# First graph's step tables built between the blocks of the first projection

## The chip, the cores and the metric

The kernel runs on one core of a Trainium2 chip. The metric is the device time of one execution, in microseconds (us); the kernel before has a median of 3173.57 us over three runs.

## The reference, cut to what matters

Two layers of a graph network on 3125 nodes with 256 features. In the first half of layer 0 the node features are normed, projected to q, k, v, and used both for an attention over 53125 sorted edges and for a mixer whose per-head k and v are normed over 64 features.

```python
edge_index = jnp.stack([src, dst])
xn = _layernorm(x, axis=-1)
x = x + _L0_gnn_ref(xn, edge_index, Wq, bq, Wk, bk, Wv, bv, Ws, bs) + _L0_mix_ref(xn[None], Wqkv, Wout, bout)[0]
...
# in _L0_gnn_ref
alpha = jnp.einsum('ehc,ehc->eh', q[dst], k[src]) / jnp.sqrt(jnp.float32(C))
amax = jax.ops.segment_max(alpha, dst, num_segments=n)
ex = jnp.exp(alpha - amax[dst])
out = jax.ops.segment_sum(msg, dst, num_segments=n)
```

The rest (an expert layer, a second graph layer, a second mixer and a gated expert layer with a second edge list) follows in order and is not touched, but for one helper that the second edge list uses too.

## The kernel before

The 3125 nodes lie as NB = 25 blocks of 128 rows in `k.X`. The sorted edges are cut into chunks of 128 and, by the block of 128 nodes to which they belong, into T1 "steps" in G1 = 4 groups of 128. For each step the kernel needs a small table: which chunk, which block, each edge's node relative to its block (`e.rel`, and as rows in memory, `e.rel_rows`), its source node (`e.src`), where a node's run of edges starts and ends (`e.flags_tab`, `e.link_tab`), and which places are void (`e.hole`). Class `Steps` makes them, and only the attention, after the projection, reads them.

Each part of the program is a `Block`: every engine has its own written-out instruction stream, and all engines meet at the Block's end. The parts at the start come in this order.

`Loads` (Block at L529): ACT issues two DMAs for x and then 28 for weights and biases. Its end is the end of the issues, not of the transfers.

`first_steps` (L295 to 326): SP loads the last node of each of the 416 chunks (`load`, L187). DVE turns it into a row of end steps (`count`), TensorE widens that row over 128 partitions (`widen`, L211), DVE compares and reduces it into chunk and block numbers (`cuts`, L242 to 252), GpSimd issues 12 indirect DMAs that fetch the edges (`gather`, L225), and SP stores and reads back the block numbers (`store`, L193, L196). DVE meanwhile takes the 25 layer statistics (`stats.block`, L469), waits for the edges and makes the flags (`mark`, L258 to 275). SP stores rows, flags and links (L199 to 205) and waits for all of them. TensorE turns two tables (`flip`, L217), and DVE keeps them (`settle`, L281 to 292).

`turn_weights` (L549 to 577): 36 weight tiles of 128x128 are transposed by TensorE and copied by DVE through eight PSUM banks. TensorE waits first for all weight loads.

`stats.finish` (L481 to 497) makes the node scales. `project0` (L586 to 784) then goes over the 25 blocks. In one turn TensorE multiplies q, k, v of a block (L694), transposes the next normed block (L677), multiplies the mixer's k and v (L704), and adds the last block to the dot products (L682). ACT squares (L632), takes a root (L635) and norms the next block (L582). DVE adds the biases into a ring of five (`qkv`, L758 and L759), keeps the transposed block (`xT`, L748), reduces the squares (L763) and scales the k heads (L770), after which it raises `heads`. GpSimd splits q in three (L664 to 668), and SP stores k and v (L647). The `Chain` class gives each DVE instruction of a chain a wait on the one before.

TensorE's q, k, v product of a block needs that block kept and the adds of the block before:

```python
pe.wait_ge(kept, b + 2)
pe.wait_ge(ab_used, b + 1)
```

The second edge list's tables are made by the same `Steps` inside `combine1` (L2361 to 2476). There `mark` stands whole between the fourth and fifth group of blocks, and TensorE's `flip` waits for it before its own fifth group.

Of the kernel before, what the change touches and what calls it, by code (L numbers as in the profile page):

```python
# [6 lines left out]
F32 = mybir.dt.float32  # L7
# [6 lines left out]
P = 128  # L14
# [141 lines left out]
class Steps:  # L156


    def __init__(self, nc, s, k, name, pairs, chunks, groups, e):
        self.nc, self.k, self.pairs, self.chunks, self.groups, self.e = nc, k, pairs, chunks, groups, e  # L160
        self.last_i = s.sb(name + "last_i", [1, chunks], I32)
        self.last_b = s.sb(name + "last_b", [1, chunks], I32)
        self.end_step = s.sb(name + "end_step", [1, chunks])
        self.below = s.sb(name + "below", [P, groups, chunks])
# [3 lines left out]
        self.here = s.sb(name + "here", [P, 2, groups, P])  # L168
        self.near = s.sb(name + "near", [P, 2, groups, P])
        self.rel_t = s.sb(name + "rel_t", [P, groups, P])  # L170
        self.rel_h = s.sb(name + "rel_h", [P, groups, P], BF)
        self.tmp = s.sb(name + "tmp", [P, groups, P])
# [3 lines left out]
        if self.block_row is None:  # L176
            self.block_row = s.sb(name + "block_row", [1, groups * P], I32)
        if e.flags_tab is not None:
            self.valid, self.starts, self.ends = (s.sb(name + x, [P, groups, P]) for x in ("valid", "starts", "ends"))
# [10 lines left out]
    def store(self, sp):  # L190
        e, groups = self.e, self.groups
# [5 lines left out]
        sp.wait_ge(self.blocked, 16)  # L197
        sp.wait_ge(self.ready, 3)
        sp.dma_start(e.rel_rows.rearrange("(g p) e -> p g e", p=P), self.rel_h[:, :, :]).then_inc(self.bdone, 16)  # L199
        sp.wait_ge(self.bdone, 32)  # L200
        if e.flags_tab is not None:
# [11 lines left out]
    def flip(self, pe):  # L213
        pe.wait_ge(self.cmp_done, 2)
        for j, x in enumerate((self.rel_t, self.here[:, 1])):
# [23 lines left out]
    def cuts(self, dve):  # L239
        v, k, c, cut, groups, chunks = self.nc.vector, self.k, self.c, self.cut, self.groups, self.chunks  # L240
        dve.wait_ge(self.spread, 1)
        c.link(v.tensor_tensor(self.below[:, :, :], wide(self.wide_end[:, 0:chunks].unsqueeze(1), [P, groups, chunks]),  # L242
                               wide(k.count_col[:, 0:groups].unsqueeze(2), [P, groups, chunks]), ALU.is_lt))
        c.link(v.tensor_reduce(cut[:, 0], self.below[:, :, :], AX.X, ALU.add))
# [10 lines left out]
    def mark(self, dve):  # L255
        v, c, here, near, tmp, rel_t, valid = self.nc.vector, self.c, self.here, self.near, self.tmp, self.rel_t, self.valid
# [7 lines left out]
        v.tensor_copy(self.rel_h[:, :, :], rel_t[:, :, :]).then_inc(self.ready, 1)  # L264
        c.link(v.tensor_scalar(valid[:, :, :], rel_t[:, :, :], 0.0, None, ALU.is_ge))
        c.link(v.tensor_scalar(tmp[:, :, :], rel_t[:, :, :], float(P), None, ALU.is_lt))
        c.link(v.tensor_tensor(valid[:, :, :], valid[:, :, :], tmp[:, :, :], ALU.mult))
        for flags, j in ((self.starts, 0), (self.ends, 1)):
            c.link(v.tensor_tensor(tmp[:, :, :], here[:, 0], near[:, j], ALU.not_equal))
            c.link(v.scalar_tensor_tensor(out=flags[:, :, :], in0=tmp[:, :, :], scalar=RESET, in1=valid[:, :, :],  # L270
                                          op0=ALU.mult, op1=ALU.mult))
        if self.e.flags_tab is not None:
            for j, x in enumerate((self.starts, self.ends)):
                v.tensor_reduce(self.link[:, j], x[:, :, :], AX.X, ALU.min).then_inc(self.flagged, 1)
        dve.sem_inc(self.cmp_done, 1)

    def settle(self, dve):
        v, c, e, groups = self.nc.vector, self.c, self.e, self.groups
# [3 lines left out]
        if e.step_row is not None:  # L282
# [4 lines left out]
            c.link(v.tensor_tensor(e.step_row[:, :, U:], duo[:, 1], duo[:, 0], ALU.subtract))  # L287
        if e.hole is not None:
# [4 lines left out]


def first_steps(nc, k, pairs, e, stats, got_x):  # L295

    with Scope(nc) as s:
        st = Steps(nc, s, k, "s1_", pairs, C1, G1, e)
        with nc.Block() as block:
            @block.sync  # L300
            def _(sp):
                st.load(sp)
                st.store(sp)

            @block.tensor
            def _(pe):
                st.widen(pe)
                st.flip(pe)

            @block.gpsimd  # L310
            def _(pool):
                st.gather(pool)

            @block.vector
            def _(dve):
                st.count(dve)
                st.cuts(dve)
                dve.wait_ge(got_x, 32)
                for b in range(NB):
                    stats.block(b)  # L320
                st.mark(dve)
                st.settle(dve)
                stats.end(dve)
# [177 lines left out]
class Loads:  # L501


    def __init__(self, nc, s, k, pj, a):
# [3 lines left out]
        self.got_x, self.got_w, cleared = (s.sem(q) for q in ("got_x", "got_w", "cleared"))  # L508
# [40 lines left out]
def turn_weights(nc, k, pj, ld):  # L549

    with Scope(nc) as s:
# [7 lines left out]
        with nc.Block() as block:  # L559
            @block.sync  # L560
            def _(sp):
                sp.wait_ge(ld.got_x, 32)

# [9 lines left out]
            def _(dve):  # L573
                for j, (_x, y) in enumerate(jobs):
                    dve.wait_ge(turned, j + 1)
                    nc.vector.tensor_copy(y, bank[j % 8][:, 0:P]).then_inc(kept, 1)
                dve.wait_ge(kept, len(jobs))

# [7 lines left out]
def project0(nc, k, pj, q_parts, kv_tab):  # L586
# [5 lines left out]
    with Scope(nc) as s:  # L592
# [22 lines left out]
        out = [s.sem(f"p0_out{j}") for j in range(B5)]  # L615
        K8 = MH // 2
        with nc.Block() as block:
# [34 lines left out]
            def _(pool):  # L652
                pool.sem_inc(parted, B5)
                pool.wait_ge(zeroed, 2)
                for i in range(0, NB // B5):
# [5 lines left out]
                    for j in range(B5):  # L661
# [7 lines left out]
                        pool.sem_inc(parted, 1)  # L669

            @block.tensor
            def _(pe):
# [14 lines left out]
                def turn(i, last=False):  # L687
                    for j in range(B5):
# [19 lines left out]
                        product((j - 1) % B5)  # L708
                pe.sem_inc(turned, B5)
# [17 lines left out]
            def _(dve):  # L727
# [22 lines left out]
                def turn(i, first=False, last=False):  # L750
                    c = Chain(dve, chain, i * (PER * B5))
                    for j in range(B5):
# [18 lines left out]
                        dve.sem_inc(heads, 1)  # L771
                    assert c.n == PER * B5
# [2341 lines left out]
def program(nc, a, out):  # L3114
    with Scope(nc) as s:
# [12 lines left out]
        with Scope(nc) as g:  # L3128
            e1 = Graph(g, "e1_", G1, streamed=True)
            with Scope(nc) as t:  # L3130
                q_parts = t.sb("q_parts", [P, NB, 3, D], BF)
                with Scope(nc) as t2:
                    pj = Projection(t2)
                    stats = LayerStats(nc, t2, k, "n0_")
                    with Scope(nc) as t3:
                        ld = Loads(nc, t3, k, pj, a)
                        first_steps(nc, k, a["pairs"], e1, stats, ld.got_x)
                        turn_weights(nc, k, pj, ld)
                    stats.finish()
                    project0(nc, k, pj, q_parts, kv_tab)  # L3140
# [101 lines left out]
```

## Time and profile before

| | |
|---|---|
| median of 3 runs | 3173.57 us (3168.86 to 3176.24) |
| span of the profiled execution | 3169.3 us |
| TensorE, VectorE (DVE), ScalarE (ACT), GpSimd (POOL) busy | 2325.7, 2011.6, 1372.1, 1774.3 us |
| mean granted TensorE clock | 0.856 |
| projection loop, first product to last | about 106.8 to 312 us |

The span runs from the first to the last instruction of one execution, which lies inside the range of the timed runs. Start times in the timeline count from the span's start. A bracket behind a row is the idle time of the engine ahead of it, and what ended it.

### The profile page before, as it was taken

The numbers are of one execution on the slowest core, as the hardware profiler recorded it, in microseconds if no ns is written. First come the engines' busy times: TensorE is split into PE (matmuls) and PEld (weight loads), VectorE is DVE, ScalarE is ACT, GpSimd is POOL, SyncE is SP. The second block draws the span as 40 slices with busy tenths as digits, with TensorE's granted clock in tenths as the row PEclk, the third lists the DMA queues.
The fourth block names the chain that finished last, engine by engine and source line by source line (L and its number), as shares of the span: only waits on it lengthen the run. The fifth ranks groups of instructions, "written<-read, shape, count | busy, mean of one in ns | idle before, by whom it ended". The sixth has DMA issues, their size and how long they took to land. (4 is left out here: it accounts for less than half of the span.)

```text
span 3169.3 us, 41063 instructions
## 1 busy us (share of the span) xinstructions
PE 2325.7 (73%) x11127; PEld 1529.8 (48%) x11128; DVE 2011.6 (63%) x4060; ACT 1372.1 (43%) x3793; POOL 1774.3 (56%) x1789
## 2 busy tenths in 40 slices
PE   0798677777776667669968667777777888888781
PEld 0454455555554556246623323333325676777660
DVE  3444799999998888100136399989995642222588
ACT  0122555655653344311126388888883222222230
POOL 1244788877874125657763377777772057777100
PEclk9899788888888655789979798989998779999895
DMA  5000677667762100034312133333331121111105
GB/s 122 21 34 30 201 206 204 202 205 205 201 204 65 55 18 27 11 111 124 89 50 64 53 97 100 100 102 100 100 94 17 28 57 36 36 36 36 16 1 173
DMA packets 163816, 287.79 MB, mean 91 GB/s; under 512 B 55320, under 2 KB 99357, under 8 KB 163598
## 3 DMA queue, kind: packets, MB, share of 16 engines
q0 software_dynamic: 79568, 187.15, 22.1%
q1 hardware_dynamic: 68628, 75.89, 7.9%
q10 hardware_dynamic: 15402, 22.14, 2.0%
q8 instruction: 102, 1.67, 0.2%
q14 instruction: 116, 0.95, 0.1%
HBM read 248.79 MB, written 36.25 MB: 90 GB/s over the span
## 5 line engine op out<-in xcount | busy, mean ns | idle before, releaser
L2273 POOL DMA_INDIRECT cv_x<-x_tab,e_src x440 | 447.8, 1018 | 197.5 <-issue 91.1
L2286 PE MATMUL cv_ps<-cv_msg,cv_hot 128*128 128x512 f32 x880 | 433.9, 651 | 167.0 <-DVE acc L2336 131.8
L913 POOL DMA_INDIRECT at_kv<-kv_tab,e_src x440 | 472.4, 1074 | 146.4 <-issue 92.0
L2707 POOL DMA_INDIRECT gs_h<-h_tab,fc_q x312 | 296.8, 951 | 178.1 <-issue 93.3
L2286 PEld LDWEIGHTS cv_ps<-cv_msg,cv_hot 128*128 128x128 f32 x880 | 179.2, 210 | 421.4 <-ACT cv_msg L2299 203.3
L1957 POOL DMA_INDIRECT pairs<-gating_pair,gating_place x288 | 278.4, 967 | 158.5 <-issue 68.9
L2299 ACT ACTIVATE cv_msg<-cv_x,factors 128x64 f32<-128x64 f32 x1320 | 356.5, 333 | 0.0
L2336 DVE TENSOR_TENSOR acc<-acc,cv_ps 128x256 f32 x880 | 307.4, 416 | 37.1 <-PE cv_ps L2286 30.5
L2297 ACT ACTIVATE cv_msg<-cv_x,factors 128x256 f32<-128x256 f32 x440 | 217.7, 495 | 130.6 <-DMA cv_x<-x_tab,e_src 130.6
L1049 PE MATMUL at_a<-at_kv,at_hot_e 128*128 128x264 f32 x880 | 251.3, 415 | 7.0 <-DVE at_kv L1122 5.0
L1024 PE MATMUL at_q<-q_parts,at_hot_n 128*128 x1320 | 217.3, 318 | 41.0 <-DVE at_kv L1106 32.2
L2668 ACT ACTIVATE gs_x_hid<-gs_x_h,x_b 128x128 f32<-128x128 f32 x320 | 91.2, 368 | 301.9 <-PE gs_x_h L2635 301.9
L2645 PE MATMUL gs_x_y<-x_w,gs_x_hid 128*128 128x256 f32 x640 | 160.4, 402 | 61.1 <-DVE gs_y L2675 57.5
L1024 PEld LDWEIGHTS at_q<-q_parts,at_hot_n 128*128 128x128 bf16 x1320 | 142.4, 110 | 106.8 <-issue 58.1
L2788 DVE TENSOR_REDUCE gs_as_dst<-gs_d 128x32 f32<-128x96 f32 x39 | 10.1, 258 | 280.0 <-DMA gs_h<-h_tab,fc_q 280.0
L1049 PEld LDWEIGHTS at_a<-at_kv,at_hot_e 128*128 128x128 f32 x880 | 165.9, 209 | 37.2 <-issue 7.3
L1133 DVE TENSOR_TENSOR acc<-acc,at_a 128x528 f32 x220 | 154.2, 701 | 36.1 <-PE at_a L1049 30.2
L2645 PEld LDWEIGHTS gs_x_y<-x_w,gs_x_hid 128*128 128x128 f32 x640 | 122.5, 199 | 82.4 <-ACT gs_x_hid L2668 55.8
L1106 DVE TENSOR_TENSOR at_kv<-at_kv,at_q 128x512 f32<-128x512 f32 x220 | 147.2, 680 | 18.2 <-DMA at_kv<-kv_tab,e_src 9.3
L2635 PE MATMUL gs_x_h<-xnT,x_w 128*128 128x128 f32 x1280 | 156.4, 279 | 0.0
L2635 PEld LDWEIGHTS gs_x_h<-xnT,x_w 128*128 128x128 f32 x1280 | 153.1, 195 | 2.1
L975 ACT ACTIVATE at_away_e<-count_row,e_rel 128x128 f32<-128x128 f32 x440 | 139.0, 386 | 0.1
(548 smaller groups left out, 4601.6 us busy)
## 6 DMA issues: line engine op xcount, KB each, us to landing
x_w<-in_L_ffn_w SPq DMA_DIRECT2D x16, 1024.0 KB, 7.7
at_rel_row<-e_rel_rows SPq DMA_DIRECT2D x55, 256.0 KB, 4.7
experts_out<-gs_y ACTq DMA_DIRECT2D x20, 512.0 KB, 2.7
x_y<-experts_out SPq DMA_DIRECT2D x20, 512.0 KB, 4.8
at_kv<-kv_tab,e_src POOLq DMA_INDIRECT x440, 3.9
cv_x<-x_tab,e_src POOLq DMA_INDIRECT x440, 2.8
kv_tab<-p_qkv SPq DMA_DIRECT2D x25, 256.0 KB, 2.0
gs_h<-h_tab,fc_q POOLq DMA_INDIRECT x312, 2.4
```

What stands on the lines that cost most here:

```text
L913: nc.gpsimd.indirect_dma_start(out=kv[:, t % (RING * Q4), 0:2 * D], out_offset=None, in_=kv_tab, in_offset=bass.IndirectOffsetOnAxis(ap=e. ...
L1024: ins = nc.tensor.matmul(ps_q[dd % 3][:, u, :], hot_n[:, t // Q4 % NHOT, t % Q4 * P:(t % Q4 + 1) * P], q_parts[:, ds(b, 1), n, :].rearrang ...
L1049: nc.tensor.matmul(to, hot_e[:, t // Q4 % NEDGE, t % Q4, :], kv[:, t % (RING * Q4), D:2 * D + H1], start=(u == 0), stop=(u == 1), skip_gro ...
L1957: nc.gpsimd.indirect_dma_start(out=pairs, out_offset=bass.IndirectOffsetOnAxis(ap=place_i[:, c:c + 1], axis=0), in_=pair[:, c, :], in_offs ...
L2273: nc.gpsimd.indirect_dma_start(out=xg[:, i % RT, u, :], out_offset=None, in_=x_tab, in_offset=bass.IndirectOffsetOnAxis(ap=e.src[:, t:t + ...
L2286: nc.tensor.matmul(ps[u % R][:, :], hot[:, i % 2, u, :], msg[:, i % 2, u, :], start=True, stop=True).then_inc(summed, 1)
L2297: nc.scalar.activation(msg[:, h, u, 0:D], xg[:, i % RT, u, :], ACT.Copy, scale=factor[:, t:t + 1, 0])
L2299: ins = nc.scalar.activation(msg[:, h, u, D + m * M:D + (m + 1) * M], xg[:, i % RT, u, 0:M], ACT.Copy, scale=factor[:, t:t + 1, 1 + m])
L2336: v.tensor_tensor(row, row, ps[u % R][:, n * D:(n + 1) * D], ALU.add).then_inc(added, 1)
L2635: ins = self.nc.tensor.matmul(self.ps_h[e % 2][:, f * P:(f + 1) * P], self.x1.w1[:, e, c, f * P:(f + 1) * P], self.xnT[:, c, b * P:(b + 1) ...
L2645: ins = self.nc.tensor.matmul(self.ps_y[e % 2][:, 0:D], self.hid[:, e % 2, f, :], self.x1.w2[:, e, f, :], start=(f == 0), stop=(f == FX // ...
L2707: nc.gpsimd.indirect_dma_start(out=hg[:, i % RT, u, :], out_offset=None, in_=h_tab, in_offset=bass.IndirectOffsetOnAxis(ap=e.src[:, i * U ...
```

## The change

The `first_steps` Block is gone. `turn_weights` takes the 25 statistics at its head on DVE, with a wait for each of five loads of x (six DMAs, for the last block is short), and then the copies. The table work moves into `project0`: `load` at the head of SP's stream, and pieces of the rest behind named blocks of each engine's loop.

The helper's methods are cut up (`cuts` into two, `mark` into four, `settle` into two, `store` into three). `mark` no longer copies three of its four columns of edges to float tiles: it reads the integer columns in place. Some tiles share memory.

```diff
-                act.dma_start(k.X[:, 0:NB - 1, :], a["x"][0:(NB - 1) * P, :].rearrange("(b p) d -> p b d", p=P)).then_inc(got_x, 16)
-                act.dma_start(k.X[0:LAST, NB - 1, :], a["x"][(NB - 1) * P:N, :]).then_inc(got_x, 16)
+                for g in range(NB // B5):
+                    lo, hi = g * B5, min(g * B5 + B5, NB - 1)
+                    act.dma_start(k.X[:, lo:hi, :], a["x"][lo * P:hi * P, :].rearrange("(b p) d -> p b d", p=P)).then_inc(got_x[g], 16)
+                act.dma_start(k.X[0:LAST, NB - 1, :], a["x"][(NB - 1) * P:N, :]).then_inc(got_x[NB // B5 - 1], 16)
...
 # turn_weights, DVE
+                for b in range(NB):
+                    if b % B5 == 0:
+                        dve.wait_ge(ld.got_x[b // B5], 32 if b // B5 == NB // B5 - 1 else 16)
+                    stats.block(b)
...
 # mark
         dve.wait_ge(self.got, 48 * self.groups)
-        v.tensor_copy(near[:, 0], self.edges[0][:, :, :, 0])
-        v.tensor_copy(near[:, 1], self.edges[2][:, :, :, 0])
-        v.tensor_copy(here[:, 1], self.edges[1][:, :, :, 1])
-        c.link(v.tensor_copy(here[:, 0], self.edges[1][:, :, :, 0]))
-        c.link(v.tensor_tensor(rel_t[:, :, :], here[:, 0], wide(self.cut[:, 5].unsqueeze(2), [P, self.groups, P]), ALU.subtract))
+        v.tensor_copy(self.from_node[:, :, :], self.edges[1][:, :, :, 1])
+        c.link(v.tensor_tensor(rel_t[:, :, :], self.edges[1][:, :, :, 0], wide(self.cut[:, 5].unsqueeze(2), [P, self.groups, P]), ALU.subtract))
...
+AT_COUNT, AT_CUTS, AT_MARK = 1, 5, 11
...
 # project0, SP, after the store of block b
+                steps.load(sp)                       # ahead of the loop
+                        if b == AT_CUTS + 2:
+                            steps.store_blocks(sp)
+                        if b == AT_MARK + 1:
+                            steps.store_rows(sp)
+                        if b == AT_MARK + 4:
+                            steps.store_flags(sp)
 # GpSimd, after the split of block b
+                        if b == AT_CUTS + 1:
+                            steps.gather(pool)
 # TensorE, after the dot products in block b
+                        if b == AT_COUNT + 2:
+                            steps.widen(pe)
+                        if b == AT_MARK + 5:
+                            steps.flip(pe)
 # DVE, after it has raised heads for block b
+                        if b == AT_COUNT:
+                            steps.count(dve)
+                        if b == AT_CUTS:
+                            steps.cuts_begin(dve)
+                        if b == AT_CUTS + 1:
+                            steps.cuts_end(dve)
+                        if b == AT_MARK:
+                            steps.mark_rows(dve)
+                        if b == AT_MARK + 1:
+                            steps.mark_valid(dve)
+                        if b == AT_MARK + 2:
+                            steps.mark_flags(dve, 0)
+                        if b == AT_MARK + 3:
+                            steps.mark_flags(dve, 1)
+                        if b == AT_MARK + 6:
+                            steps.settle_rows(dve)
+                        if b == AT_MARK + 7:
+                            steps.settle_holes(dve)
```

## Rows read from the trace of the kernel before

**Rows 1.** Timeline of the loads: start us, us, engine, line, what was issued

```profile
5.75 0.43 ACTq L533 DMA_DIRECT2D X<-in_x  x1
...
29.88 0.64 SPq L187 DMA_DIRECT2D s_last_i<-in_pairs  x1
```

**Rows 2.** Busy time by stretch, the 30th microsecond; last two columns DMA share, GB/s

```profile
29.00:30.00 1.00, 0.00 (x0) 0.00 (x0) 0.00 (x0) 0.00 (x0) 0.00 (x0) 1.00 0.13 28
```

**Rows 3.** Timeline of DVE in first_steps (each row may end in its wait)

```profile
35.42 0.58 DVE L237 TENSOR_TENSOR s_end_step<-s_end_step,count_row 1x416 f32<-1x416 f32 x1
...
37.84 1.89 DVE L242 TENSOR_TENSOR s_below<-s_turned,count_col 128x1664 f32<-128x1664 f32 x1 [1.84 <-PE s_turned L211]
39.77 1.89 DVE L244 TENSOR_REDUCE s_cut<-s_below 128x4 f32<-128x1664 f32 x1
...
42.66 0.16 DVE L252 SCALAR_TENSOR_TENSOR s_cut<-s_cut 128x4 f32<-128x4 f32 x1
42.86 8.26 DVE L469 BATCH_NORM_STATS2 n_parts<-X 128x6 f32<-128x256 f32 x25
...
59.97 0.43 DVE L258 CAST s_near<-s_edges 128x512 f32<-128x512 int32 x1 [8.85 <-DMA s_edges<-in_pairs,e_chunk]
...
67.06 0.69 DVE L274 TENSOR_REDUCE s_link<-s_starts 128x4 f32<-128x512 f32 x1
```

**Rows 4.** Waits of SP's queue up to 110 us: us in total, times, longest

```profile
SPq L299 <- DMA e_link<-s_link: 12.6, 1, 12.6
...
SPq L196 <- DMA s_block_of_step<-s_block_i: 9.7, 1, 9.7
```

**Rows 5.** Timeline of turn_weights and the first instruction of stats.finish

```profile
83.54 3.65 PE L570 MATMUL turn_bank<-ident,mix_kv 128*128 128x128 f32 x16 [14.42 <-PEq L299]
...
89.11 2.46 DVE L576 COPY fcT<-turn_bank 128x128 f32<-128x128 f32 x12
...
92.09 0.20 DVE L487 TENSOR_TENSOR n_t<-n_parts 128x25 f32<-128x25 f32 x1 [0.52 <-PEq L559]
```

**Rows 6.** Line L763 by itself: ns min/median/max, first and last start us

```profile
L763 DVE TENSOR_REDUCE p_st<-p_sq x25: 1219/1220/1221, 117.1 to 307.0; 128x16 f32<-128x1024 f32 x25
```

**Rows 7.** Timeline of one block of the projection

```profile
127.81 0.44 PE L677 MATMUL p_t<-ident,p_xn 128*128 128x128 f32 x2 [0.38 <-ACT p_xn L582]
128.19 3.67 PE L704 MATMUL p_m<-mix_kvT,p_xT 128*128 128x512 f32 x8
...
129.15 0.41 DVE L748 COPY p_xT<-p_t 128x256 f32<-128x256 f32 x1
...
132.59 1.88 PE L694 MATMUL p_a<-Wqkv,p_xT 128*128 128x512 f32 x4
...
132.96 1.22 DVE L763 TENSOR_REDUCE p_st<-p_sq 128x16 f32<-128x1024 f32 x1 [3.40 <-ACT p_sq L632]
```

**Rows 8.** Busy time by stretch: PE, PEld, DVE, ACT, POOL; clock, DMA share, GB/s

```profile
104.00:112.00 8.00, 7.38 (x12) 3.41 (x13) 0.43 (x1) 0.00 (x0) 0.00 (x0) 0.50 0.00 0
...
128.20:136.10 7.90, 7.52 (x27) 4.04 (x27) 3.86 (x8) 2.21 (x4) 3.61 (x5) 1.00 0.09 33
```

**Rows 9.** TensorE's flip in first_steps, its first half

```profile
67.15 1.11 PE L217 MATMUL s_turned<-ident,s_rel_t 128*128 128x128 f32 x4 [29.34 <-DVEq L275]
```

**Rows 10.** Line L225, the gathers on GpSimd: ns min/median/max, first and last start

```profile
L225 POOL DMA_INDIRECT s_edges<-in_pairs,e_chunk x12: 946/946/1104, 42.4 to 56.3; - x12
```

**Rows 11.** Timeline of the attention: a GpSimd gather and a DVE product beside it

```profile
360.07 1.22 DVE L1122 TENSOR_TENSOR at_kv<-at_kv 128x1024 f32<-128x1024 f32 x1
360.25 1.87 POOL L913 DMA_INDIRECT at_kv<-kv_tab,e_src  x1 [0.31 <-issue]
```

**Rows 12.** Timeline of the second edge list's mark and flip

```profile
2480.95 0.34 DVE L258 CAST s_near<-s_edges 128x384 f32<-128x384 int32 x1
...
2482.14 0.56 DVE L262 TENSOR_TENSOR s_rel_t<-s_here,s_cut 128x384 f32<-128x384 f32 x1
...
2486.82 0.90 PE L217 MATMUL s_turned<-ident,s_rel_t 128*128 128x128 f32 x3 [6.66 <-DVEq L275]
```

More of the change, by code:

```diff
@@ L176, in __init__ @@
         if self.block_row is None:
-            self.block_row = s.sb(name + "block_row", [1, groups * P], I32)
+            self.block_row = row
         if e.flags_tab is not None:
-            self.valid, self.starts, self.ends = (s.sb(name + x, [P, groups, P]) for x in ("valid", "starts", "ends"))
+            self.valid = own_valid
+            self.starts, self.ends = (s.sb(name + x, [P, groups, P]) for x in ("starts", "ends"))
         self.turned = [s.ps(name + f"turned{j}", [P, 512]) for j in range(2)]
@@ L190, in store, with store_blocks @@
     def store(self, sp):
-        e, groups = self.e, self.groups
+        self.store_blocks(sp)
+        self.store_rows(sp)
+        self.store_flags(sp)
+    def store_blocks(self, sp):
+        groups = self.groups
         sp.wait_ge(self.ready, 2)
@@ L197, in store, with store_rows @@
         sp.wait_ge(self.blocked, 16)
+    def store_rows(self, sp):
+        e = self.e
         sp.wait_ge(self.ready, 3)
@@ L200, in store, with store_flags @@
         sp.wait_ge(self.bdone, 32)
+    def store_flags(self, sp):
+        e = self.e
         if e.flags_tab is not None:
@@ L214, in flip @@
         pe.wait_ge(self.cmp_done, 2)
-        for j, x in enumerate((self.rel_t, self.here[:, 1])):
+        for j, x in enumerate((self.rel_t, self.from_node)):
             for g in range(self.groups):
@@ L255, in mark, with mark_rows, mark_valid @@
     def mark(self, dve):
[L256 to L262 removed]
+        self.mark_rows(dve)
+        self.mark_valid(dve)
+        for j in range(2):
+            self.mark_flags(dve, j)
+    def mark_rows(self, dve):
+        v, c, rel_t = self.nc.vector, self.c, self.rel_t
+        dve.wait_ge(self.got, 48 * self.groups)
+        v.tensor_copy(self.from_node[:, :, :], self.edges[1][:, :, :, 1])
+        c.link(v.tensor_tensor(rel_t[:, :, :], self.edges[1][:, :, :, 0], wide(self.cut[:, 5].unsqueeze(2), [P, self.groups, P]), ALU.subtract))
         v.tensor_copy(self.rel_h[:, :, :], rel_t[:, :, :]).then_inc(self.ready, 1)
+    def mark_valid(self, dve):
+        v, c, tmp, rel_t, valid = self.nc.vector, self.c, self.tmp, self.rel_t, self.valid
         c.link(v.tensor_scalar(valid[:, :, :], rel_t[:, :, :], 0.0, None, ALU.is_ge))
@@ L267, in mark, with mark_flags, settle_rows @@
         c.link(v.tensor_tensor(valid[:, :, :], valid[:, :, :], tmp[:, :, :], ALU.mult))
[L268 to L271, printed above, removed]
+    def mark_flags(self, dve, j):
+        v, c, tmp, valid = self.nc.vector, self.c, self.tmp, self.valid
+        flags = (self.starts, self.ends)[j]
+        c.link(v.tensor_tensor(tmp[:, :, :], self.edges[1][:, :, :, 0], self.edges[2 * j][:, :, :, 0], ALU.not_equal))
+        c.link(v.scalar_tensor_tensor(out=flags[:, :, :], in0=tmp[:, :, :], scalar=RESET, in1=valid[:, :, :],
+                                      op0=ALU.mult, op1=ALU.mult))
         if self.e.flags_tab is not None:
-            for j, x in enumerate((self.starts, self.ends)):
-                v.tensor_reduce(self.link[:, j], x[:, :, :], AX.X, ALU.min).then_inc(self.flagged, 1)
-        dve.sem_inc(self.cmp_done, 1)
+            v.tensor_reduce(self.link[:, j], flags[:, :, :], AX.X, ALU.min).then_inc(self.flagged, 1)
+        if j == 1:
+            dve.sem_inc(self.cmp_done, 1)
     def settle(self, dve):
+        self.settle_rows(dve)
+        self.settle_holes(dve)
+    def settle_rows(self, dve):
         v, c, e, groups = self.nc.vector, self.c, self.e, self.groups
@@ L292, in settle @@
             c.link(v.tensor_scalar(e.hole[:, :], e.hole[:, :], LOW, None, ALU.mult))
[L295 to L323, printed above, removed]
 def segment_softmax(nc, k, name, groups, heads, score, valid, starts, ends, scale, x1, xnT):
@@ L507, in __init__ @@
         self.fc = [s.sb(f"fc{j}", [P, KC, D]) for j in range(3)]
-        self.got_x, self.got_w, cleared = (s.sem(q) for q in ("got_x", "got_w", "cleared"))
+        self.got_x = [s.sem(f"got_x{g}") for g in range(NB // B5)]
+        self.got_w, cleared = s.sem("got_w"), s.sem("cleared")
         got_x, got_w = self.got_x, self.got_w
@@ L577, in _ @@
                 dve.wait_ge(kept, len(jobs))
+                stats.end(dve)
 def normed_block(nc, k, act, b, slot, sem):
```

37 lines of the change are left out of this document (21 added, 16 removed).

## The prediction, on record before the result

> **What bounds the kernel now.** The page's chain of waits covers only the last part of the span, so I read the start of the program: first the timeline, then the waits of SP's queue, then busy time by stretch. No engine is near full over the whole span, so what counts is which event opens each stretch.
>
> The loads' part ends when SP starts its first DMA, at 29.9 us [rows 1]. By then the transfers are nearly through: in the 30th microsecond the DMA engines are 13% busy [rows 2]. From 29.9 to 83.5 us the tables of the first graph are built, one dependent step after another. DVE is idle 8.85 us for the gathered edges [rows 3], and at the end all engines wait for SP, which waits 12.6 us for the link stores [rows 4]. Only the 25 statistics (8.26 us, [rows 3]) are work that the projection needs. TensorE starts the weight tiles at 83.54, DVE ends them at 89.11 + 2.46 = 91.57, and the node scales start at 92.09 [rows 5].
>
> The projection is a loop with a fixed pitch: (307.0 - 117.1) / 24 = 7.91 us [rows 6]. TensorE is busy 7.52 us in such a stretch, at clock 1.00 (2.4 GHz), and idle 0.38 us a block, waiting for the normed block; DVE is busy 3.86 and GpSimd 3.61 of 7.90 us [rows 7, 8]. TensorE bounds the loop, closely followed by the chain product, square, reduce, root, norm, transpose. DVE and GpSimd have half of each block free.
>
> **Part 1: the removed Block.** Start of the node scales after the change, built up:
>
> - Loads end. ACT issues four DMAs more, at most 4 x 0.43 = 1.7 us [rows 1]. The bytes are the same, and they fill the time to the 29th microsecond anyway, so the lower bound is 0. I take 0.5: the issues run beside the transfers. 29.9 + 0.5 = 30.4.
> - Statistics: 8.26 us, to 38.7. The five waits on x cost nothing: x was issued first, and all transfers are nearly done at 30 [rows 2]. For the same reason the split of x gains nothing, since the statistics cannot start before the loads' Block ends.
> - Weight tiles: before, 91.57 - 83.54 = 8.03 us from TensorE's first transpose to DVE's last copy [rows 5]. Now TensorE fills the eight banks while DVE takes the statistics, so only the copies are left: the last 12 took 2.46 us, 0.205 each, and 36 x 0.205 = 7.4. Bounds 7.4 and 8.0. I take 7.5, to 46.2.
> - The Block's end, 0.52 us as before [rows 5], to 46.7.
>
> Gain: 92.1 - 46.7 = 45.4 us (bounds 43.7 and 46.0).
>
> **Part 2: DVE's pieces in the loop.** A piece stands behind `heads` and ahead of the next adds. The adds, the copy of the transposed block and then a wait of 3.40 us follow [rows 7]. A piece of length L moves the adds and the copy by L. The copy ends at 129.15 + 0.41 = 129.56, and TensorE wants it for L694 at 132.59, so L is free up to 3.0 us, and up to 3.4 with TensorE's own 0.38. The reduction behind it allows 3.4 too. The pieces, from [rows 3]: count, four instructions of at most 0.58, under 2.4; first half of the cuts, 1.89; second half, from 39.77 to 42.82, 3.05; rows of the mark, one cast of 0.43, one two-input pass of 0.69 and one cast, 1.6; validity, 1.6; flags, three passes of 0.69 each time, 2.1 twice; settle, four passes of at most 0.69, under 2.8, and 1.6 for the holes. Together about 18.6 us, and all are under the limit; only the second half of the cuts comes to it (0 to 0.2 us). Reading integer columns in place of float ones is not shown before. Below, nothing changes; above, it doubles a pass of 0.69, and the flags' piece comes to 2.8, still free. I take 0.1 us for all of part 2. If the cover were gone, the price would be 18.6 us.
>
> **Part 3: TensorE's pieces.** Here only 0.38 us a block is free. Widen is one product of 416 columns. L694 takes 1.88 us for two products of 512 columns at the full clock [rows 7], so 0.94 x 416/512 = 0.76, and 0.76 - 0.38 = 0.4 us. Flip is eight transposes. Its two halves before took about 1.1 us each [rows 9], 2.2 in all after a long idle time; in the loop two transposes take 0.44 [rows 7], 1.8 for eight. Lower bound half of 2.2. I take 1.7 - 0.38 = 1.3 us. Together 1.7 (1.1 to 2.5).
>
> **Part 4: GpSimd's and SP's queues.** The 12 gathers stand behind the split of block 6 and wait for the chunk numbers, some 2.3 us after DVE's `heads` of block 6 (call it time 0). They take (56.3 - 42.4) + 0.95 = 14.9 us [rows 10], and the data came 59.97 - 57.3 = 2.7 us after the last [rows 3]: at 20 us. DVE asks for them behind block 11, at 5 x 7.91 = 39.6. Margin 19 us. Behind them wait the splits of blocks 7 and on. Split 7 starts 13 us late, and GpSimd gains 7.9 - 3.6, less gaps about 3.8 us, a block, so it is level again by block 12. The ring of five `qkv` buffers asks for split 7 only before the adds of block 12, again at 39.6, and it is done at 21.4. Cost 0.
>
> SP stops behind the store of block 7 for the block numbers, 9.7 us and then a second small transfer [rows 4], and behind block 15 for flags and links, 12.6 us. The stores of k and v queued behind are wanted five blocks on, 39.6 us. Cost 0. The first load is wanted two blocks into the loop. Cost 0.
>
> **Part 5: the second edge list.** Its mark has DVE run while TensorE waits 6.66 us for it [rows 12]. Four casts take 2482.14 - 2480.95 = 1.19 us, and one of about 0.37 stays. Gain 0.8 us, 0 if integer reads are slower.
>
> **Sum against the profiled execution:** -45.4 + 0.1 + 1.7 - 0.8 = -44.4 us, a span of 3169.3 - 44.4 = 3124.9. The median of the runs is 3173.57, 4.3 above that span, so the time forecast is 3129.2 us. All behind the loop is moved forward whole, since it is released by the Block ends only.
>
> **Rivals.**
>
> *A, the gathers are held up.* In the attention a gather issue that begins beside a DVE product of two tiles takes 1.87 us and not 0.95 [rows 11]. At 1.87 each, 12 take 26 us, which is still inside the margin of part 4. It decides from (14.9 + 19) / 12 = 2.8 us a gather. At three times the pitch, 3.8 us, they take 45 us, DVE waits some 12 us behind block 11, and the time is 3141. Against it: the gathers of the first graph ran beside the 25 statistics at 0.946 median [rows 10], and the loop's long DVE instructions read PSUM or one tile. The Trainium skill, page "SBUF — State Buffer", section "SBUF: two separate sides", says that DVE and GpSimd share a port pair which one holds for a whole instruction, two-input or two-port, so that descriptors starve; it quotes 3,100 ns for a transfer that takes 620 alone. By that factor of five (an estimate) the gathers would take 75 us and more than 30 us would be lost; the attention's rows show a factor of two, so the rule holds in kind and not in that size. Chance 0.04.
>
> *B, the pieces are not covered.* If DVE's idle time ahead of the reduction cannot be used, because the adds that now come late feed TensorE after all, 18.6 us come back: 3148. For it: every piece delays the adds. Against it: the 3.0 us worked out above. Chance 0.05.
>
> *C, slower.* At clock 0.50 TensorE is busy 7.38 of 8 us and finishes less than one block [rows 8]. If the new pauses or the earlier start hold the loop at 1.2 GHz, a block costs about 7.1 us more, the doubling of its bound. From 45 / 7.1 = 6.3 blocks on the change is a loss; with ten blocks it is 3200. For it: TensorE now pauses while DVE takes the statistics, right before. Against it: before, it had been idle for 14.42 us ahead of the tiles too [rows 5], and the loop still rose from 0.50 to 1.00 [rows 8]. Chance 0.02.
>
> *D, no gain.* The time before 83 us is not the tables' but the transfers', and the tile work waits for the weights at that hour anyway. Against it: DMA at 28 GB/s from 29 us on. It would give 3173. Chance 0.01.
>
> *E, drift of the rest.* 2850 us lie behind the loop, with a clock that moves between levels and gathers that collide; the three runs before differ by 7.4 us. More than 10 us from the sum by this alone: 0.08.
>
> The forecast has 0.80. Range: the runs' own spread of about 4 us on either side, with the bounds of parts 1, 3 and 5 (some 2.5 us), gives 3122 to 3136. I widen it upwards towards A, to 3140, and down to 3119 for drift, which leaves out at most 2 in 10. A measurement of this kernel tells about 0.2%, 6.3 us, from no change: faster 0.95, same 0.02, slower 0.03.
>
> **What the profile after would show.** Statistics from about 30 us, eight transposes while they run, copies done near 46, node scales at 46.7. Loop pitch 7.91 but for blocks 3 and 16, longer by 0.4 and 1.3, and perhaps 7. No DVE wait on the edges behind block 11. The attention starts some 44 us earlier. Wrong would be a pitch of 10 us at the blocks with pieces (B), a DVE wait for the edges (A), clock 0.50 in mid-loop (C), or TensorE's first transpose later than 39 (D).

## The result and the profile after

The changed kernel takes 3130.76 us in the median (3124.3 to 3134.4), the kernel before 3174.16 beside it. The ratio is 0.9862, 95% interval 0.9848 to 0.9877, so 43 us or 1.4% faster. The forecast was 3129.2 with a range of 3119 to 3140, and 0.95 on faster. The profiled execution has a span of 3127.2, against 3169.3 before: 42.1 us less, where the sum gave 44.4.

The start of the program, which answers to [rows 1], [rows 3] and [rows 5], reads like this in the timeline of the changed kernel:

```profile
5.76 4.13 ACTq L541 DMA_DIRECT2D X<-in_x  x5
9.92 1.54 ACTq L542 DMA_DIRECT2D X<-in_x  x1
...
30.36 8.27 DVE L474 BATCH_NORM_STATS2 n_parts<-X 128x6 f32<-128x256 f32 x25 [24.64 <-PEq L535]
33.61 1.97 PE L574 MATMUL turn_bank<-ident,mix_kv 128*128 128x128 f32 x8 [33.61 <-DMA gat_rows<-in_L_ffn_ln_beta]
38.54 3.24 DVE L584 COPY mix_kvT<-turn_bank 128x128 f32<-128x128 f32 x16
...
43.28 2.46 DVE L584 COPY fcT<-turn_bank 128x128 f32<-128x128 f32 x12
...
46.28 0.20 DVE L492 TENSOR_TENSOR n_t<-n_parts 128x25 f32<-128x25 f32 x1 [0.54 <-PEq L567]
...
49.01 0.65 SPq L189 DMA_DIRECT2D s_last_i<-in_pairs  x1
```

The statistics start at 30.36, eight transposes lie under them, and the node scales start at 46.28 instead of 92.09. SP's first load of the tables now starts at 49.01, at the head of the loop. TensorE's bracket shows that the last weight load landed at 33.6, still 4.9 us ahead of the first copy.

The loop is not as even as in [rows 6]. That line's summary is now

```profile
L789 DVE TENSOR_REDUCE p_st<-p_sq x25: 1219/1220/1220, 70.4 to 264.6; 128x16 f32<-128x1024 f32 x25
L790 DVE TENSOR_SCALAR p_st<-p_st x25: 174/175/662, 71.6 to 265.9; 128x16 f32<-128x16 f32 x25
L793 DVE TENSOR_TENSOR p_st<-p_st x25: 166/168/553, 72.1 to 266.4; 128x8 f32<-128x8 f32 x25
```

The columns are minimum, median and maximum in ns. The loop takes 194.25 us between first and last reduction, 4.4 more than the 189.85 before. And two small DVE instructions, on tiles of 16 and 8 elements, sometimes take up to 0.66 and 0.55 us instead of 0.17. Such an instruction is called held from here on. Before, neither ever was; the first of them:

```profile
L764 DVE TENSOR_SCALAR p_st<-p_st x25: 174/175/176, 118.4 to 308.2; 128x16 f32<-128x16 f32 x25
```

The block after the first piece (the count, which delays the adds by 1.6 us) shows it. First DVE, then GpSimd, of the changed kernel:

```profile
86.17 1.22 DVE L789 TENSOR_REDUCE p_st<-p_sq 128x16 f32<-128x1024 f32 x1 [1.78 <-ACT p_sq L645]
87.43 0.66 DVE L790 TENSOR_SCALAR p_st<-p_st 128x16 f32<-128x16 f32 x1
88.13 0.25 DVE L792 RECIPROCAL p_st<-p_st 128x16 f32<-128x16 f32 x1
```

```profile
86.50 0.67 POOL L687 TENSOR_TENSOR p_part<-p_rest,p_part 128x256 bf16<-128x256 f32 x1
87.24 0.82 POOL L688 COPY q_parts<-p_part 128x768 bf16<-128x768 bf16 x1
```

GpSimd's copy runs from 87.24 to 88.06. DVE's scalar pass starts at 87.43 and ends at 88.09, right behind it. Before, the copy came 1.6 us earlier in the block and was over by then: it started 0.57 us ahead of the reduction of [rows 7] at 132.96, where it now starts 1.07 behind the reduction.

```profile
132.39 0.82 POOL L668 COPY q_parts<-p_part 128x768 bf16<-128x768 bf16 x1
```

The piece has moved the adds, and with them GpSimd's split.

The intervals between the starts of the reductions (interval 2 is the one behind the reduction of block 2, counted from 0), read from the timeline, against 7.91 us throughout before:

| interval behind reduction | us | what lies there |
|---|---|---|
| 2 | 8.41 | GpSimd late from the count in block 1; L790 held to 0.66 |
| 3 | 8.21 | the widening on TensorE |
| 6 | 8.15 | late from the first half of the cuts; L793 0.41 |
| 9, 10 | 8.50, 8.20 | GpSimd works off what waited behind the gathers |
| 12, 13, 14, 15 | 8.10, 8.37, 8.25, 8.26 | late from the four pieces of the mark |
| 16 | 8.00 | the flip on TensorE |
| 18, 19 | 8.51, 8.36 | late from the two pieces of the settling |
| 7 | 7.93 | late from the second half of the cuts, 3.06 us; GpSimd gathers, so no split lies beside it |
| all others | 7.90 to 7.91 | |

Without the widening and the flip (0.30 and 0.09) that is 4.0 us, all of it, but for the 0.02 of interval 7, in blocks with a held instruction.

Busy time by stretch of the changed kernel, the loop and then the part behind it (`mixer_matrix0`, until the attention's first gather); columns as in [rows 8]:

```profile
70.30:264.60 194.30, 181.46 (x632) 98.24 (x630) 113.28 (x224) 52.65 (x97) 98.70 (x133) 1.00 0.18 45
264.60:283.00 18.40, 10.70 (x32) 7.96 (x32) 6.70 (x15) 0.67 (x2) 0.42 (x2) 0.72 0.00 0
```

The loop holds the high clock throughout, the part behind it does not. TensorE's last 16 products there, at L803 of the kernel before and L847 of the changed one:

```profile
L803 PE MATMUL g<-g_t,mix_q x16: 378/380/484, 318.0 to 321.4; 128*128 128x256 f32 x16
```

```profile
L847 PE MATMUL g<-g_t,mix_q x16: 379/634/796, 275.2 to 280.6; 128*128 128x256 f32 x16
```

Their starts spread over 5.4 us instead of 3.4: most ran at the lower clock. From the last reduction to the attention's first gather it is 18.3 us instead of 16.7.

The ledger, each point a start in the two traces: node scales 92.09 to 46.28, gain 45.8; first reduction 117.1 to 70.4, gain 46.8; last reduction 306.98 to 264.61, gain 42.4; first gather of the attention 323.7 to 282.9, gain 40.8; end 42.1. The extra 1.0 us ahead of the first reduction is the clock: in the loop's first block it rises about 2 us sooner. It isn't steady: from the node scales to the first reduction it is 25.1 us before and 24.1 here, but 25.2 to 25.3 in the traces with the mark earlier, with short pieces and with both edits below. The row 17 to 19 us behind the start of the node scales, in the kernel before and in the changed one:

```profile
109.00:111.00 2.00, 2.00 (x4) 0.86 (x4) 0.00 (x0) 0.00 (x0) 0.00 (x0) 0.50 0.00 0
```

```profile
63.20:65.20 2.00, 2.00 (x6) 1.12 (x5) 0.00 (x0) 0.00 (x0) 0.00 (x0) 0.71 0.00 0
```

### The profile page after: what moved, and what is told of

It is laid out like the page before. It is cut to its first block and busy times, and to the rows that moved or that the text cites. A ratio compares the mean times of both kernels' runs of the same rounds, so it can differ in the third digit from the quotient of the medians.

```text
span 3127.2 us, 41052 instructions
## 1 busy us (share of the span) xinstructions
PE 2330.7 (75%) x11127; PEld 1529.1 (49%) x11128; DVE 2012.7 (64%) x4054; ACT 1372.7 (44%) x3793; POOL 1767.1 (57%) x1789
```

## The experiments

### One more DVE instruction in each block of the kernel before

```diff
                         dve.sem_inc(heads, 1)
+                        v.tensor_reduce(drag[:, :, :], pj.mix_kvT[:, :, 0:768].unsqueeze(2), AX.X, ALU.add).then_inc(dragged, 1)
+                        dve.wait_ge(dragged, b + 1)
```

> The kernel before, with one more DVE reduction of about 1.8 us behind heads in each of the 25 blocks. Theory of the held instruction: GpSimd's split of q starts after the adds, so it starts 1.8 us later, and its copy lies over the small DVE instructions L764 and L767 of the next turn, which wait for its end. These grow from 0.17 to 0.4 to 0.7 us, and the pitch from 7.91 to 8.3 to 8.6 us, 10 to 17 us in all. Rival, cover alone: 1.8 us is below the 3.0 us that DVE has free, so the pitch stays 7.91 and the time within 2 us of before. Rival, no cover: pitch 9.7, 45 us more.

Measured: 3192.4 us, ratio 1.0056 (1.0040 to 1.0073). The pitch is 8.50 us in 22 of 24 intervals, 0.59 more for 1.75 us added. The last reduction moves from 306.98 to 320.16, 13.2 us; most of the rest of the 18 us lies in later parts of the program and is taken up below. One block of this kernel:

```profile
158.67 1.22 DVE L765 TENSOR_REDUCE p_st<-p_sq 128x16 f32<-128x1024 f32 x1 [1.68 <-ACT p_sq L634]
159.10 0.67 POOL L669 TENSOR_TENSOR p_part<-p_rest,p_part 128x256 bf16<-128x256 f32 x1
159.83 0.82 POOL L670 COPY q_parts<-p_part 128x768 bf16<-128x768 bf16 x1
159.92 0.76 DVE L766 TENSOR_SCALAR p_st<-p_st 128x16 f32<-128x16 f32 x1
160.72 0.25 DVE L768 RECIPROCAL p_st<-p_st 128x16 f32<-128x16 f32 x1
```

DVE still waits 1.68 us for ACT ahead of the reduction, so the added time itself is covered. What grows is the scalar pass: it runs from 159.92 to 160.68, just past the end of the copy at 160.65. It stands on the chain square, reduce, root, norm, transpose that paces the loop.

### The same without GpSimd's split

The five instructions L664 to L668 are left out of each block, and `q_parts` is set to zero once ahead of the loop; the attention's scores come from zeros.

> As the one with the added 1.8 us reduction, but GpSimd's five instructions that split q are left out of each block (q_parts is only set to zero once, so the scores are all from zeros). Theory of the held instruction: with no GpSimd work in the loop nothing holds DVE, pitch 7.91. If the added length itself, or the later adds, cost TensorE time, the pitch stays at what the run with the split shows.

```profile
L762 DVE TENSOR_REDUCE p_st<-p_sq x25: 1219/1220/1220, 125.4 to 315.2; 128x16 f32<-128x1024 f32 x25
```

(315.2 - 125.4) / 24 = 7.91. The added 1.75 us cost nothing once GpSimd is silent. The start is 8 us later because the zeroing comes first.

### The same with half the length

```diff
+                        v.tensor_reduce(drag[:, :, :], pj.mix_kvT[:, :, 0:336].unsqueeze(2), AX.X, ALU.add).then_inc(dragged, 1)
```

> The kernel before, with an added DVE reduction of about 0.85 us in each block. Before, GpSimd's copy ends 0.26 us past the start of the next reduction, and the first small instruction that can be held starts at 1.25. So 0.85 us later it ends at 1.1, still ahead. Theory of the held instruction: pitch 7.91, no cost, a threshold at about 1.0 us. If the cost grows in proportion to the added length, the pitch is about half way to that of the 1.8 us run.

```profile
L765 DVE TENSOR_REDUCE p_st<-p_sq x25: 1219/1220/1221, 116.7 to 306.6; 128x16 f32<-128x1024 f32 x25
```

Pitch 7.91. The time is 3173.43 us in one run, that of before. A block of it shows why: the copy is over at 157.41, and the scalar pass starts at 157.59.

```profile
156.59 0.82 POOL L670 COPY q_parts<-p_part 128x768 bf16<-128x768 bf16 x1
157.59 0.17 DVE L766 TENSOR_SCALAR p_st<-p_st 128x16 f32<-128x16 f32 x1
```

So the cost isn't proportional: 0 at 0.85 us, 0.59 at 1.75, and both lie well below the 3.4 us that are free. With the run without the split, which has the same added length and the same late adds and no cost, this rules out the length and the late adds as causes. What is left is the work that GpSimd does beside the small passes.

### The changed kernel without GpSimd's split

The edit is that of the second experiment, on the changed kernel; the scores again come from zeros.

> The changed kernel without GpSimd's split of q in the loop (q_parts set to zero once). Theory of the held instruction: the loop's 4.4 us over 24 x 7.91 shrink to TensorE's own, about 0.3 at the widening and 0.1 to 0.6 at the flip, under 1 us in all. If the pieces' length or TensorE's pieces are the cost, 3 us or more stay.

The intervals are 8.21 behind reduction 3 and 8.00 behind 16, 7.98 behind 8, where a gather issue lies beside a scalar pass of 0.25 us, and all others 7.90 to 7.92. So the widening costs 0.30 and the flip 0.09, and the other 4.0 us are gone. The whole time, 3138.32 us in one run, can't be compared, as the zeroing puts the loop about 10 us later.

### The order alone, tables whole

`first_steps` stays whole and stands behind `turn_weights`, which takes the statistics at its head.

```diff
-                        first_steps(nc, k, a["pairs"], e1, stats, ld.got_x)
-                        turn_weights(nc, k, pj, ld)
+                        turn_weights(nc, k, pj, ld, stats)
+                        first_steps(nc, k, a["pairs"], e1, stats, ld.got_x)
```

> Only the order of the change: statistics and weight tiles right behind the loads, and the tables' part whole behind them, nothing in the loop. The tables' part took 53 us before, with the 8.26 us of statistics hidden under its gathers. Theory, the gain is all from the tables leaving the path: node scales start at 46 + 54 = 100 us instead of 92.1, some 7 to 8 us slower than before, 3181 us. Rival, the gain is in taking the statistics and tiles early: this would be faster than before.

3183.05 us, ratio 1.0031 (1.0014 to 1.0047), slower. The node scales start at 97.90, 5.8 us later than before. DVE now waits 16.84 us for the edges where it waited 8.85 and had the statistics besides [rows 3]:

```profile
74.81 0.43 DVE L258 CAST s_near<-s_edges 128x512 f32<-128x512 int32 x1 [16.84 <-DMA s_edges<-in_pairs,e_chunk]
...
97.90 0.20 DVE L483 TENSOR_TENSOR n_t<-n_parts 128x25 f32<-128x25 f32 x1 [9.99 <-PEq L299]
```

The whole gain is from taking the tables off the path; the new order by itself loses, since the statistics no longer lie under the gathers.

### The four pieces of the mark behind one block

```diff
-                        if b == AT_MARK + 1:
+                        if b == AT_MARK:
                             steps.mark_valid(dve)
```

and the same for both calls of `mark_flags`.

> The changed kernel with the four pieces of the mark behind one block (11) instead of four. They are 7.3 us together. Theory, 3.4 us a block are free: the interval from block 11 to 12 grows by 3.9 us to about 11.8, with a held small instruction of 0.3 to 0.6 in the next, and blocks 12 to 14 return to 7.91. If DVE had no cover the interval would be 15.2; if the whole length were free, 7.91.

The interval is 11.50: 3.6 us more, for 7.04 us by which the adds came late. So 3.45 us were free, as worked out. The next one is 9.30 and not 8.2 to 8.5. The view of waits shows that DVE waits there once more, for TensorE's product:

```profile
DVE p_qkv L784 <- PE p_b L716: 1.5, 1, 1.5
```

TensorE had stood still for 3.93 us, for the late copy, and its granted clock fell to the lower level (1.2 GHz). The four products that follow, and the busy time by stretch around them:

```profile
171.05 3.54 PE L716 MATMUL p_a<-Wqkv,p_xT 128*128 128x512 f32 x4 [3.93 <-DVE p_xT L774]
```

```profile
171.00:174.60 3.60, 3.55 (x5) 1.68 (x6) 2.63 (x5) 0.70 (x2) 3.30 (x5) 0.55 0.35 109
```

They take 3.54 us instead of the 1.88 of [rows 7], at a mean clock of 0.55; from 174.6 us on it is 1.00 again. These 1.66 us more account for the 1.4 by which the interval is too long. A held instruction, 0.39 us for 0.17, lies there too, but TensorE was the later of the two. Blocks 13 to 15 are at 7.90 to 7.91, as expected. The last reduction is at 268.35, 3.7 us behind the changed kernel's.

### The mark four blocks earlier

```diff
-AT_COUNT, AT_CUTS, AT_MARK = 1, 5, 11
+AT_COUNT, AT_CUTS, AT_MARK = 1, 5, 7
```

> The changed kernel with the mark behind block 7 instead of 11, so four blocks earlier, and what hangs on it. The gathers end 20 us after block 6, 12 us after block 7, by part 4 of the prediction. Theory: DVE waits there for the edges, and the interval from block 7 to 8 grows by 12 + 1.6 - 3.4, about 10 us. If the margin of part 4 is larger than worked out, less; with no wait the interval is 7.91.

```profile
129.97 0.69 DVE L796 TENSOR_TENSOR p_kv<-p_m,p_st 128x512 f32<-128x512 f32 x1 [0.33 <-ACT p_st L648]
142.65 0.43 DVE L284 CAST s_from_node<-s_edges 128x512 f32<-128x512 int32 x1 [11.99 <-DMA s_edges<-in_pairs,e_chunk]
142.99 1.16 DVE L285 TENSOR_TENSOR s_scratch<-s_edges,s_cut 128x512 f32<-128x512 int32 x1
```

DVE waits 11.99 us, and the interval is 18.58, 10.7 more. The block before raises `heads` at 122.7, so the edges come 19.9 us later, as part 4 had it (20). The two passes of the mark that follow the wait stretch, too (1.16 for 0.69, 0.93 for 0.43), for GpSimd is splitting beside them. The next interval is 10.37, longer too, and for the same reason as with the whole mark. TensorE stood still for 11.0 us, and its first four products took 3.78 us instead of 1.88. A stretch of that time:

```profile
145.00:149.00 4.00, 2.58 (x3) 1.18 (x4) 3.56 (x9) 0.49 (x2) 2.65 (x4) 0.50 0.31 98
```

### x in two loads

> The changed kernel with x in two loads as before. Theory: the five loads gain nothing, since the statistics start at the end of the loads' part, and cost up to 0.5 us of issue time: statistics start at 29.9 instead of 30.4, all behind it 0.5 us earlier. If the split of x mattered, the statistics would start or end later here, by some us.

The edit puts the two DMAs of before back, with one wait for both.

```profile
29.90 8.27 DVE L474 BATCH_NORM_STATS2 n_parts<-X 128x6 f32<-128x256 f32 x25 [24.18 <-PEq L535]
...
45.82 0.20 DVE L492 TENSOR_TENSOR n_t<-n_parts 128x25 f32<-128x25 f32 x1 [0.54 <-PEq L565]
```

Both start 0.46 us earlier. The time is 3131.92 us in one run: the five loads gain nothing and cost 0.46 us, which the whole time can't show.

### Short pieces

The same DVE instructions stand here one to four behind each of 21 blocks, at most about 1.0 us a block but for the two passes of 1.89 and the last piece of 1.6, which lies behind the last block. The flip, SP's stores and x in two loads go with it, as the expectation says. In excerpt:

```diff
+        if b == 11:
+            c.link(v.tensor_tensor(rel_t[:, :, :], self.edges[1][:, :, :, 0], wide(cut[:, 5].unsqueeze(2), [P, groups, P]), ALU.subtract))
...
+        if b == 14:
+            c.link(v.tensor_tensor(valid[:, :, :], valid[:, :, :], tmp[:, :, :], ALU.mult))
```

> The changed kernel with DVE's pieces cut to at most about 1.0 us, one or two instructions behind each of 20 blocks (but the two passes of 1.89 us, behind blocks 4 and 5), the flip behind block 13 and the flags' stores behind block 21, and x in two loads. Theory of the held instruction: below 1.0 us nothing is held, so what stays of the loop's 4.4 us over 24 x 7.91 is the widening 0.3, the flip 0.1, about 0.25 each behind blocks 4 and 5, and 0.9 behind blocks 9 and 10, where GpSimd works off the gathers: 1.8 us, so the loop is 2.6 us shorter than after the change, and the issue of x saves 0.5. About 3 us under the changed kernel, 3128. Rival, cost by the total length of the pieces: the loop stays at 4.4 over.

The intervals are longer by 0.30 at the widening, 0.09 at the flip, 0.23 and 0.22 behind the two long passes, 0.18, 0.90 and 0.28 behind reductions 8, 9 and 10, and nothing elsewhere. The 0.18 stand where a gather issue holds a scalar pass (shown in the last section). That is 2.2 us over 24 x 7.91, near the 1.8 expected, against 4.4. The last reduction is at 263.16, only 1.4 us ahead of the changed kernel's: the clock rose later here, and the first reduction came at 71.1 instead of 70.4. The whole time is 3130.88 us (3128.55 to 3134.87), ratio to before 0.9859 (0.9838 to 0.9880).

### The changed kernel once more

> The changed kernel once more, unaltered, beside the one with short pieces: 3131, a loop 4.4 us over 24 x 7.91.

3132.01 us (3123.28 to 3137.09), ratio 0.9854 (0.9832 to 0.9876), with loop intervals within 0.04 us of the first trace's and 4.2 us over 24 x 7.91. The 2 us that the short pieces gain in the loop can't be seen in whole times.

### The pieces behind the copy

```diff
                             keep(b + 1, (j + 1) % B5)
+                        if b - 1 == AT_COUNT:
+                            steps.count(dve)
...
                         dve.wait_ge(squared, b + 1)
```

> The changed kernel with every DVE piece behind the copy of the transposed block instead of ahead of the adds. The adds are then on time, and GpSimd's split starts on time, but the pieces run beside it. Theory of the held instruction: casts, one-input passes of SBUF and two-input passes of the pieces and the split's instructions hold each other, so pieces and split both stretch, and a piece over about 2.5 us delays the reduction; the loop's excess is between 2 and 7 us. If only the late adds were the cost, the excess would be TensorE's 0.4 us alone.

The loop takes 2.1 us over 24 x 7.91, of which 1.3 stand behind reductions 9 and 10 and 0.4 at widening and flip. GpSimd's copy of block 1 takes 1.07 us instead of 0.82 and the pieces stretch (the four passes of the count take 0.73 to 0.94 and not 0.37 to 0.58), but both lie in DVE's and GpSimd's free time. The time is 3125.7 us in one run. Here the 16 products behind the loop ran at the high clock:

```profile
L847 PE MATMUL g<-g_t,mix_q x16: 378/379/484, 273.3 to 276.7; 128*128 128x256 f32 x16
```

### Both edits

> The changed kernel with both edits that the runs favour: the pieces behind the copy of the transposed block, and x in two loads. Theory: node scales start 0.4 us earlier (45.8), the loop's excess over 24 x 7.91 is 2.2 us instead of 4.4, together 2.6 us under the changed kernel, 3128 to 3129 us; the attention starts about 280. It stays open whether the tail behind the loop runs at the high clock (another 1.7 us).

3127.17 us (3119.46 to 3141.44), ratio to before 0.9854 (0.983 to 0.9878). The node scales start at 46.02 (expected 45.8) and the loop has 2.1 us over 24 x 7.91 (expected 2.2). The 16 products behind the loop ran at the lower clock, and the first gather of the attention starts at 281.4, 1.5 us ahead of the changed kernel's. It is the lowest median of those with several runs, but the interval is that of the changed kernel. The traces show a shorter loop; the whole times can't tell the two kernels apart.

## Why the prediction was right

**Part 1, the removed Block** (45.4): 45.8 measured. Statistics at 30.36 against 30.4, copies done at 45.74 against 46.2, since DVE took 7.2 us for 36 and not 7.5. The four DMAs more cost 0.46 us, as the run with two loads shows, against 0.5. The split of x gained nothing, as said. Rival D is out: the last weight load had landed at 33.6, and the node scales did come 45.8 us earlier.

**Part 2, DVE's pieces** (0.1): 4.0 us measured. This is the term that was mis-sized, and its step was "all are under the limit". The limit itself, 3.4 us, holds: 3.45 in the run with the whole mark. What was missing is GpSimd. I had counted what waits for the adds on TensorE and DVE, and on GpSimd only the ring of five buffers. But a split that runs 1.6 us later lies over the small DVE passes, and these are held until GpSimd's instruction ends. The two runs with 1.75 us added, with and without the split, and the one with 0.85 us, show it. The mechanism was in rival A, from [rows 11], but I had looked for it only at the gathers. The Trainium skill, page "SBUF — State Buffer", section "SBUF: two separate sides", says that DVE and GpSimd take a shared port pair for a whole instruction and the other blocks fully, where the DVE pass is in a two-port mode, or has two SBUF inputs and the GpSimd instruction reads SBUF. Here a DVE pass of 16 elements beside a GpSimd copy ended 0.03 us behind the copy's end, so the trace agrees; which ports are held, no run shows. The pieces listed in part 2 add up to 19.1 us, not 18.6, and in the trace they take 18.0; no forecast but rival B's price hangs on it.

**Part 3, TensorE's pieces** (1.7): 0.39 measured, 0.30 and 0.09. The widening delayed the next product by 0.89 us (94.30 to 95.19) and the flip by 0.87 (199.82 to 200.69), where I had 0.76 and 1.7. The flip was mis-sized because the 0.44 us of two transposes includes the end of the second one: four take 0.44 us from the first start to the start of what follows (199.82 to 200.26), so eight cost 0.87. Free were 0.6 to 0.8 us, not 0.38. The 0.38 was the idle time of the products alone; in the same turn of the kernel before, the transposes' weight loads had 0.78 idle. That these loads set the limit is argued and not tested. The two errors of parts 2 and 3 partly cancel: 1.8 in all against 4.4.

**Part 4, the queues** (0): right. Gathers from 124.5 to 138.5, no wait behind block 11, and the edges 19.9 us after block 6 in the run with the early mark. SP waited 8.7, 3.2 and 7.8 us, and no block had a wait on its stores. What the gathers did cost is the 0.9 us behind reductions 9 and 10, by the split that caught up. **Rival A** did not come: the 12 gathers took 0.95 us each but for a first one of 1.14, and 15.0 us in all. Its worst case, a factor put on the gather's own time, was also the wrong form. In the attention of the kernel before, all 54 issues that were lengthened, to between 1.31 and 2.02 us, ended 0.82 to 0.86 us behind the end of the DVE product beside them. The delay is set by what is left of that DVE pass.

**Part 5, the second edge list** (0.8): TensorE waits 5.73 us at the flip instead of the 6.66 of [rows 12], 0.9 gained. The pass that reads integer columns takes 0.56 us for 384 elements, as with float:

```profile
2445.76 0.56 DVE L298 TENSOR_TENSOR s_scratch<-s_edges 128x384 f32<-128x384 int32 x1
...
2448.20 0.90 PE L230 MATMUL s_turned<-ident,s_scratch 128*128 128x128 f32 x3 [5.73 <-DVEq L304]
```

**What the sum did not have.** The clock: 1.0 us gained in the loop's first blocks, 1.6 lost behind the loop. With them the ledger closes: 45.8 + 1.0 - 4.4 - 1.6 = 40.8, as at the first gather. Part 5 makes it 41.7 of the 42.1 at the end, and the last 0.4 are within the drift below. The 16 products ran at the high clock in the kernel before, with both added reductions beside GpSimd's split, with the order alone and with the pieces behind the copy, and wholly or partly at the low one in the other traces. What decides it stays open; no run was made for it.

**The rest of the program** does drift, as rival E has it: from the second layer's statistics (1072.1 before, 1031.7 after) to the end it is 2097.2 us before, 2095.5 after, 2098.9 in its repeat, and 2092.2 to 2103.5 in the eleven other traces. So some 11 us of span come and go with nothing changed there. The 2103.5 are those of the run with 1.75 us added, 6 us over the kernel before, and make up most of what its time has beyond the 13 us of its loop. All four of its runs are that slow, so it need not be chance from run to run; no run here tells what sets it. Against this drift, that the total came within 1.6 us of the forecast is in part luck, as is that part 2's 3.9 us too little were met by 1.3 too much in part 3.

**Rival C** did not come: the loop's clock is 1.00 after the first blocks. But it is near. With the mark whole or too early, TensorE stood still for 3.93 and 11.0 us in mid-loop, and the clock fell in both, as their runs show. In the changed kernel each piece stayed under the free time, and TensorE had no such pause. **Rival B** did not come either; with it, each piece would have cost its length, where the reduction of 0.85 us cost nothing.

## What to carry to other kernels

Work moved into an engine's free time is covered only if what it delays is looked at on every engine that waits for it, and then on the engines beside which that work now lands. Measure the cover in the trace by a dummy of two lengths: a cost in proportion to the length points to missing cover, one that sets in below the free time (here between 0.85 and 1.75 us of 3.4) to an overlap, and leaving out the neighbour's work tells which. Keep each piece under the free time. Past it the excess is paid in full (3.6 us for 7.04), and here the pause also cost TensorE its clock for a while, 1.4 us more. A wait that all engines share is worth far more than the pieces cost: 53 us of tables became 4 us of loop.

## What the runs showed of the hardware

A DVE scalar pass of 16 elements took 0.76 us instead of 0.17 beside a GpSimd copy of 128x768 bf16, and ended 0.03 us behind it. A pass with two inputs of 8 elements was held to 0.55. In all 14 traces, every one of these two passes that was lengthened beyond 0.21 us beside GpSimd's split ended 0.02 to 0.03 us behind the end of a GpSimd instruction, a copy or a subtraction. The reciprocal between them and the reduction of 1024 elements kept their 0.25 to 0.26 and 1.22 us in all blocks of the changed kernel, also when GpSimd was busy. A gather issue can hold the scalar pass, too, but more briefly. In the run with short pieces one that started 0.60 us into a gather issue took 0.34 us and ended with it:

```profile
135.81 0.94 POOL L238 DMA_INDIRECT s_edges<-in_pairs,e_chunk  x1 [0.30 <-issue]
136.42 0.34 DVE L853 TENSOR_SCALAR p_st<-p_st 128x16 f32<-128x16 f32 x1
```

One that started 0.20 us into an issue took 0.17, one that started 0.04 us ahead of an issue took 0.25 (the changed kernel without the split), and 0.17 is also what was taken by passes with two inputs of 8 elements that started 0.42 us (changed kernel) and 0.69 us (short pieces) into one.

The hold goes both ways: GpSimd's copy took 1.16 us instead of 0.82 beside the mark's passes in the run with the early mark. TensorE's granted clock fell from 1.00 to the lower level when it stood still for 3.93 us in mid-loop, and the same four products then took 3.54 us instead of 1.88.
